# Two states per partition in a selective scan: half blocks, column-half sums and residuals on TensorE, on one Trainium2 core

## What is computed

```python
h = _L0_tok_ref(log_dt, Lambda, x, 1024)          # (64, 128, 1024): a kernel of 1024 lengths per head
h = concatenate([h, txt], axis=1)                 # (64, 205, 1024)
h = h + attn(layernorm(h))
h = h + ffn(layernorm(h))

def attn(x):                                      # selective scan, 16 states per channel
    A = -exp(A_log)                               # (1024, 16)
    xp = einsum('bld,rd->blr', x, x_proj_w)       # 32 for dt, 16 for B, 16 for C
    dt = softplus(einsum('blr,dr->bld', xp[..., :32], dt_proj_w) + dt_proj_b)
    # for each l:  h = exp(dt * A) * h + dt * B * x ;  y = sum over the 16 states of h * C
    return y + D * x

def ffn(x):                                       # weights are looked up, 4 bits or 8 bits by row norm
    return where(norm(x) > 64, x @ w8.T, x @ w4.T) + bias
```

## Time and profile before

| | us |
|---|---|
| median of 3 runs | 6210.84 (6210.68 to 6211.06) |
| profiled execution | 6212.96 |
| its span | 6211.1 |
| PE busy | 5793.1 (93%) |
| POOL busy | 5709.9 (92%) |
| DVE busy | 5698.9 (92%) |
| ACT busy | 5123.3 (82%) |

### The profile page before, as it was taken

One profiled execution on the slowest core, in us unless ns is written; L12 is line 12 of the kernel. 1 busy time (PEld: TensorE's weight loads), 2 busy tenths in 40 slices (PEclk: granted clock), 3 DMA queues, 4 the chain that ended last, 5 costly groups with the idle time before them and its releaser, 6 DMA issues. The chain is left out here.

```text
span 6211.1 us, 111922 instructions
## 1 busy us (share of the span) xinstructions
PE 5793.1 (93%) x35091; PEld 5384.9 (87%) x35091; DVE 5698.9 (92%) x4564; ACT 5123.3 (82%) x12831; POOL 5709.9 (92%) x3484
## 2 busy tenths in 40 slices
PE   4676999999999999999999999999999999999998
PEld 3545899999999999999999999999999999999997
DVE  8776999999999999999999999999999999999996
ACT  5716888888888888888888888888888888888884
POOL 4526999999999999999999999999999999999995
PEclk9887999999999999999999999999999999999999
DMA  4701221222122211222122212221222112221220
GB/s 94 160 2 66 83 82 61 77 88 87 60 77 86 88 71 68 83 88 77 61 83 88 82 62 77 88 83 61 77 88 88 68 71 83 88 77 61 83 82 34
DMA packets 115881, 478.49 MB, mean 77 GB/s; under 512 B 17441, under 2 KB 52401, under 8 KB 107122
## 3 DMA queue, kind: packets, MB, share of 16 engines
q1 hardware_dynamic: 115314, 471.10, 22.0%
HBM read 327.82 MB, written 143.24 MB: 76 GB/s over the span
## 5 line engine op out<-in xcount | busy, mean ns | idle before, releaser
L1103 POOL TENSOR_TENSOR s_ring<-s_bc,s_u_t 128x820 f32<-128x820 f32 x2048 | 3618.3, 1788 | 4.4 <-DMA s_bc<-rows_bc 4.4
L999 ACT ACTIVATE s_decay<-s_dt_t,a_neg 128x205 f32<-128x205 f32 x8192 | 3047.3, 420 | 418.4 <-DVE s_ring L1164 346.7
L895 PE MATMUL s_y_ps<-s_ring,ident 128*128 128x205 f32 x16384 | 3140.5, 341 | 115.3 <-issue 61.6
L895 PEld LDWEIGHTS s_y_ps<-s_ring,ident 128*128 128x128 f32 x16384 | 2863.3, 191 | 207.4 <-POOL s_ring L1109 115.4
L1158 DVE TENSOR_TENSOR_SCAN s_decay<-s_decay,s_ring 128x820 f32<-128x820 f32 x1216 | 2265.0, 1863 | 192.9 <-ACT s_decay L999 178.9
L1109 POOL TENSOR_TENSOR s_ring<-s_ring,s_bc 128x820 f32<-128x820 f32 x832 | 1605.3, 1929 | 78.3 <-DVE s_ring L1158 78.2
L1158 DVE TENSOR_TENSOR_SCAN s_ring<-s_decay,s_ring 128x820 f32<-128x820 f32 x832 | 1542.8, 1854 | 41.9 <-ACT s_decay L999 41.1
L928 PE MATMUL s_xch<-s_x_t,w_low 128*128 128x205 f32 x8192 | 1524.3, 338 | 0.5 <-ACT s_x_t L1042 0.2
L928 PEld LDWEIGHTS s_xch<-s_x_t,w_low 128*128 128x128 f32 x8192 | 1422.6, 190 | 35.3 <-issue 30.5
L1164 DVE TENSOR_TENSOR s_ring<-s_decay,s_bc 128x820 f32<-128x820 f32 x1216 | 1229.5, 1011 | 41.8
L889 PE MATMUL s_y_ps<-s_x_t,s_d_diag 128*128 128x205 f32 x1024 | 279.1, 354 | 35.2 <-ACT s_x_t L1037 35.2
(11 more groups left out here) (165 smaller groups left out, 4223.5 us busy)
## 6 DMA issues: line engine op xcount, KB each, us to landing
s_bc<-rows_bc SPq DMA_DIRECT2D x64, 3280.0 KB, 11.0
mixed<-t_res SPq DMA_DIRECT2D x32, 1024.0 KB, 9.6
s_x_in<-mixed SPq DMA_DIRECT2D x64, 512.0 KB
s_h<-mixed SPq DMA_DIRECT2D x64, 512.0 KB
before<-s_h SPq DMA_DIRECT2D x64, 512.0 KB
out<-s_h SPq DMA_DIRECT2D x64, 512.0 KB
s_x_in<-in_txt SPq DMA_DIRECT2D x64, 308.0 KB
s_h<-in_txt SPq DMA_DIRECT2D x64, 308.0 KB
```

The costliest lines, as they stand in the source:

```text
L895: last = nc.tensor.matmul(y_ps, ident[:, :], ring[:, c % RING, n * LEN:(n + 1) * LEN], start=False, stop=(c % 4 == 3 and n == CN - 1))
L999: last = A.activation(decay[s % 2][:, n * LEN:(n + 1) * LEN], dt_t[:, par, j, :], ACT.Exp, scale=t["a_neg"][:, j, n0 + n:n0 + n + 1])
L1103: nc.gpsimd.tensor_tensor(ring[:, s % RING, :].rearrange("p (n l) -> p n l", n=CN), bc[:, par, n0:n0 + CN, :], u_t[:, j, :].unsqueeze(1).b ...
```

## The change

1. A partition now holds one of 64 channels for one of two neighbouring states: partitions 0 to 63 the even states, 64 to 127 the odd ones. There are 16 half blocks of 64 channels and 8 pairs of states; a chunk is one half block with 4 pairs, and there are still 32 chunks of 820 columns. Chunks s and s+1 (s even) are the two half blocks of one block. `bc` has half as many rows per partition, filled by two DMAs.
2. The softplus and dt * x are computed in the old layout (`dt_n`, `u_n`), and SP copies each piece of two blocks into the new one (`dt_t`, `u_t`) by four DMAs of 64 partitions. The copy of dt leaves the first column out, which holds 1e37 from the start; `reset` is gone.
3. PE sums a pair of chunks at once, into the two column halves of the array, with a stack of two 64x64 identities as weights, one chunk later than before.
4. PE adds the residual (a product of the identity with h1) into the bank before the four transposed products, which are now products rather than transposes. ACT takes the bank to h1, for "add" with an accumulated sum, from which mean2 is made without its own pass.
5. `ON_DVE` has 23 chunks, POOL the other 9.
6. All plans, `X_ORDER` and the order of SP's queue are new.

```diff
-            sp.dma_start(t["a_neg"][:, :, :], dram["A_log"].rearrange("(j p) n -> p j n", p=P)).then_inc(alog_in, 16)
+            for i in range(2):
+                sp.dma_start(a_all[64 * i:64 * i + 64, :, :], dram["A_log"].rearrange("(b p) n -> p b n", p=64)).then_inc(alog_in, 16)
...
+PE_PLAN = {2: [("add", 0), ("ffn_late", 4)], 3: [("add", 1), ("out_low", 0)], 4: [("add", 2)], 5: [("add", 3)],
+           6: [("ffn_late", 5)], 8: [("turn1", 0)], 9: [("turn1", 1), ("ffn_late", 6)], 10: [("turn1", 2), ("turn1", 3)],
+           11: [("ffn_late", 7)], 12: [("xproj", (0, 4)), ("xproj", (4, 8))], 15: [("dt", 0)], 17: [("turn2", 0)],
+           18: [("out_low", 1), ("turn2", 1)], 20: [("dt", 1)], 22: [("out_high", 0), ("out_high", 1), ("turn2", 2)],
+           23: [("dt", 2)], 25: [("turn2", 3)], 26: [("ffn", 0), ("ffn", 1)], 28: [("dt", 3), ("ffn", 2)], 31: [("ffn", 3)]}
+ACT_PLAN = {0: [("mean1", 0)], 1: [("blk", -1), ("var1", 0)], 2: [("add", 0)], 3: [("mean1", 1), ("ffn_late", 4), ("add", 1)],
+            5: [("mean2", 0), ("out_low", 0)], 6: [("add", 2), ("var1", 1)], 7: [("blk", 0), ("norm1", 0)],
...
+            25: [("soft", (2, 1)), ("soft", (2, 2))], 26: [("blk", 5)], 27: [("ffn", 0)], 28: [("ffn", 1)],
+            29: [("soft", (3, 0))], 30: [("ffn", 2), ("soft", (3, 1)), ("blk", 6)], 31: [("soft", (3, 2)), ("ffn", 3)]}
+DVE_PLAN = {19: [("dt", 0)], 21: [("dt", 1)], 25: [("dt", 2)], 31: [("dt", 3)]}
+POOL_PLAN = {7: [("root1", 0)], 8: [("u_hi", 2)], 12: [("u_hi", 3)], 18: [("root2", 0)], 26: [("u_lo", 0)], 28: [("u_lo", 1)]}
...
+SP_ORDER = [("keep", 0), ("u_hi", 2), ("u_hi", 3), ("spread", 0), ("steps", 0), ("u_lo", 0), ("steps", 1), ("u_lo", 1),
+            ("steps", 2), ("write", 0), ("load_rows", 0), ("load", 0), ("steps", 3)]
...
-ON_DVE = (1, 3, 4, 5, 7, 9, 11, 13, 14, 15, 17, 19, 21, 23, 24, 25, 27, 29, 31)
+ON_DVE = (1, 2, 3, 5, 6, 7, 8, 9, 11, 13, 14, 15, 16, 17, 18, 19, 21, 23, 24, 27, 29, 30, 31)
...
+            def halves(target, place, source, r, first, signal):
+
+                for i in range(2):
+                    for h in range(2):
+                        sp.dma_start(target[64 * i:64 * i + 64, place + h:place + 4:2, first:],
+                                     source[64 * h:64 * h + 64, 2 * r:2 * r + 2, first:]).then_inc(signal, 16)
+
+            def steps(v, par, r):
+                wait(sp, p_empty, v * P_USES + r + 2)
+                halves(dt_t, dt_place(par, 4 * r), dt_n, r, 1, dt_in[r])
+
+            def inputs(v, r):
+                wait(sp, u_done, v * 4 + r + 1)
+                halves(u_t, 4 * r, u_n, r, 0, u_in[r])
...
                 for n in range(CN):
-                    last = nc.tensor.matmul(y_ps, ident[:, :], ring[:, c % RING, n * LEN:(n + 1) * LEN],
-                                            start=False, stop=(c % 4 == 3 and n == CN - 1))
-                last.then_inc(sum_done, 1)
+                    for h in range(2):
+                        last = nc.tensor.matmul(y_ps[sides[h], :], t["stack"][:, :], ring[:, (c + h) % RING, n * LEN:(n + 1) * LEN],
+                                                start=False, stop=(c % 4 == 2 and n == CN - 1))
+                        if n == CN - 1:
+                            last.then_inc(sum_done, 1)
...
+                nc.tensor.matmul(bank[0:rows(k), :], ident[0:rows(k), 0:rows(k)], h1[0:rows(k), par, k, 512 * side:512 * side + 512],
+                                 start=True, stop=False)
                 for j in range(4):
-                    last = nc.tensor.transpose(bank[0:rows(k), P * j:P * j + P], x_t[:, par, 4 * side + j, cols(k)], ident[:, :])
+                    last = nc.tensor.matmul(bank[0:rows(k), P * j:P * j + P], x_t[:, par, 4 * side + j, cols(k)], ident[:, :], start=False, stop=(j == 3))
...
+            def add(v, par, r, x):
+                k, side = r // 2, r % 2
+                bank, empty = take(x, "add", r)
+                A.activation(h1[0:rows(k), par, k, 512 * side:512 * side + 512], bank[0:rows(k), :], ACT.Copy,
+                             accum_out=half_sum[0:rows(k), k, side:side + 1]).then_inc(empty, 1)
```

More of the change, by code:

```diff
@@ L27 @@
 NS = 16
+NB, NK = 2 * ND, NS // 2
 RANK = 32
@@ L616, in _ @@
                 last.then_inc(turned, 1)
[L619 to L624, removed]
@@ L837, in spread @@
                 wait(sp, spread_out, v * 16 + 16)
-                sp.dma_start(bc[:, par, :, :], rows_bc[par:par + 1, :, :].broadcast_to([P, 2 * NS, LEN])).then_inc(bc_in[par], 16)
-            def entry(u, par, x, groups, ahead=True):
-                if "add" in groups:
-                    keep(u - 1, 1 - par, x)
-                if "turn1" in groups and ahead:
-                    load(u + 2, x)
-                if "turn1" in groups:
-                    spread(u + 1, 1 - par)
-                if "out_low" in groups:
-                    write(u - 2, par, x)
-                if not isinstance(u, int) or 0 <= u < BATCH:
-                    load_rows(u, par)
+                for i in range(2):
+                    sp.dma_start(bc[64 * i:64 * i + 64, par, :, :],
+                                 rows_bc[par:par + 1, i::2, :].broadcast_to([64, 2 * NK, LEN])).then_inc(bc_in[par], 16)
@@ new lines, in inputs @@
+            def inputs(v, r):
+                wait(sp, u_done, v * 4 + r + 1)
+                halves(u_t, 4 * r, u_n, r, 0, u_in[r])
+            def entry(u, par, x, groups, ahead=True):
+                for name, arg in SP_ORDER:
+                    if name == "keep" and "add" in groups:
+                        keep(u - 1, 1 - par, x)
+                    if name == "load" and "turn1" in groups and ahead:
+                        load(u + 2, x)
+                    if name == "spread" and "turn1" in groups:
+                        spread(u + 1, 1 - par)
+                    if name == "write" and "out_low" in groups:
+                        write(u - 2, par, x)
+                    if name == "load_rows" and (not isinstance(u, int) or 0 <= u < BATCH):
+                        load_rows(u, par)
+                    if name == "steps" and "turn1" in groups:
+                        steps(u + 1, 1 - par, arg)
+                    if name == "u_lo" and "turn1" in groups:
+                        inputs(u + 1, arg)
+                    if name == "u_hi" and (not isinstance(u, int) or 0 <= u < BATCH):
+                        inputs(u, arg)
@@ L884, in sums @@
                 j = c // 4
+                sides = [slice(64 * h, 64 * h + 64) for h in range(2)]
                 if c % 4 == 0:
@@ L995, in chunk @@
                     wait(act, dve_hc, u * PER_DVE + by_dve(before))
[L996 to L1000 removed]
+                if s == 0:
+                    act.wait_ge(large_set, 1)
+                if s % 8 == 0:
+                    wait(act, dt_in[s // 8], u * 64 + 64)
+                for k in range(CN):
+                    last = A.activation(decay[s % 2][:, k * LEN:(k + 1) * LEN], dt_t[:, dt_place(par, b), :], ACT.Exp,
+                                        scale=t["a_neg"][:, b, k0 + k:k0 + k + 1])
                 last.then_inc(decay_done, 1)
@@ L1008, in mean @@
                 n = rows(k)
+                minus_mean = t["ln_in"][0:n, which - 1, 0, k:k + 1]
                 if which == 1:
                     wait(act, loaded, v * 32 + 32)
+                    A.activation(xn[0:n, k, :], x_in[0:n, k, :], ACT.Copy, accum_out=ln_sum[0:n, k:k + 1]).then_inc(ln_piece[which], 1)
+                    wait(act, ln_piece[which], v * LN_DONE + PIECE[which]["mean", k, 0])
+                    A.activation(minus_mean, ln_sum[0:n, k:k + 1], ACT.Copy, scale=-1.0 / DIM).then_inc(ln_piece[which], 1)
                 else:
@@ L1032, in var, with finish @@
                 A.activation(ve, total, ACT.Identity, scale=1.0 / DIM, bias=t["eps_ln"][0:n, :]).then_inc(ln_piece[which], 1)
+            def add(v, par, r, x):
[3 more added lines that the diff above has]
+                             accum_out=half_sum[0:rows(k), k, side:side + 1]).then_inc(empty, 1)
+            def finish(name, v, par, k, x):
+                side = ("out_low", "out_high").index(name)
+                bank, empty = take(x, name, k)
+                if side == 0 and k == 0:
+                    wait(act, kept[par], (v - par) * 16 + 32)
+                A.activation(h1[0:rows(k), par, k, 512 * side:512 * side + 512], bank[0:rows(k), :], ACT.Copy).then_inc(empty, 1)
             def block_output(u, par, j, x):
```

168 lines of the change are left out of this document (77 added, 91 removed), and 6 rows, old and new, of the table ACT_PLAN.

## The result

The changed kernel takes 6716.26 us (median of 4 runs, 6713.19 to 6734.76), the kernel before 6210.76. The ratio is 1.082 (95% interval 1.0807 to 1.0833): 505 us slower, where 25 us faster was forecast, and outside the range of 6010 to 6340. The profiled execution after took 6734.76 us with a span of 6733.0.

A forecast was written before the change was run, and what follows sets the result against it. POOL was taken as the bound, 87.9 us an entry. DVE's 82.9 plus 2.0 for PE's lateness and 2.4 for the load gave 87.3; 64 entries saved 38 us, once-only costs added 13: 6185 us, range 6010 to 6340.

The forecast's parts named there:

- Engine loads: Busy time per entry after the change: DVE 82.9 us and busiest, POOL 78.3, ACT 78.9, PE 71 to 76.
- Its sums: PE's C sums in two column halves: 0.09 us a record, falling from 44.5 to 23 us an entry.
- The load of x_in: End of SP's queue: next x_in lands 1.5 us after DVE's chunk 31, idling DVE 2.4 us an entry.
- load_rows and the load behind it: Last transfers in SP's queue: 4.5 us at 367 GB/s plus 1.6 for start and landing, 6.1; slower pace 6.9.
- the eight issues ahead of the write: SP's four DMAs of u_lo 1 and four of steps 2, 0.45 to 0.54 us apart: 4.0 us.
- Rival B: SP's queue, slots 28 to 31: x_in lands at +4 or later; 6314 us at +4.0, 6371 at +4.9; chance 0.28.
- +1.7: Landing of x_in in us after DVE's chunk 31, beyond which each further us adds 64 us in total.
- +2.2: Landing of x_in in us after DVE's chunk 31 at which the entry reaches 87.9 us, deciding for Rival B.
- The other idle time: DVE idle from PE's lateness, slots 3 to 11 and 28 to 31: 2.0 us an entry, bounds 0.5 and 4.6.
- Once only: Costs outside the repeated entries: first softplus pieces +4, tail after the last scan +8, A_log load +1: +13 us.
- The clock: PE, 83% busy with short gaps, keeps its clock at 0.99 unless waits grow.
- Rival A: The load of x_in is in time: entry 84.9 us (83.5 to 85.6), total 6032 us; chance 0.28.

The follow-up runs named there:

- e5: e4 with write and load_rows moved ahead of both u_lo in SP's queue; 6158.74 us, ratio 0.9925 to the kernel before.
- e7: e5 with the C sums over the full array width, weights padded with 64 columns of zeros; 6861.07 us, ratio 1.1055.
- e3: Changed kernel with the four dt copies of steps 3 moved behind the next entry's keep, the load still late; 6616.16 us, ratio 1.0663.
- e1: Changed kernel with the load of x_in moved ahead of spread in SP's queue; 6316.58 us, ratio 1.0186.
- e4: Changed kernel with the moves of e1 and e3 together: load early, steps 3 behind the next keep; 6256.9 us, ratio 1.0081.
- e6: e5 without the residual products on PE, so the output is wrong; 6069.24 us, ratio 0.9779.
- e11: e10 with four entries in a pass of the engines' loop instead of two; 6101.3 us, ratio 0.983.
- e10: e9 with out_high 0 one slot sooner on PE, slot 21 instead of 22; 6147.9 us, ratio 0.99.
- e9: e5 with ffn_late 4 ahead of add 0 in PE's and ACT's plans and in X_ORDER; 6148.95 us, ratio 0.9904.

## Why the prediction was wrong

**Engine loads: right but for PE.** DVE, POOL and ACT came within 0.4 us an entry. PE has 81.3 us, and 79.3 in e5 with fewer stops, instead of 71 to 76. Its sums take 1718.6 / 64 = 26.9 of them in e5 where 23 was taken; which of its other terms make up the rest was not worked out. PE had room for it. (Its records were 5638 / 11.36 = 496 an entry by the earlier trace rows, not 512.) The sums come 16 records in 1.56 us, 0.10 each with the end of the last one in it, about the 0.09 taken. The Trainium skill's sentence that a weight load overlaps matmuls in flight only where the row group differs (TensorE: Matmul & The Clock Gate, Part 3) doesn't hold here: both halves use all rows, and e7 and e5 differ by 2.94 against 1.56 us for 16 records, each with its own load.

**The load of x_in: right in place, wrong in size. This is the failed step.** The step is the term "load_rows and the load behind it", 6.1 us that measured 10.75, and in second place the eight issues ahead of the write, 4.0 that measured 5.5. The terms by the rows of SP's queue above, counted from 3003.68:

| | forecast | measured |
|---|---|---|
| u_lo 1 issued | -12.9 | -12.7 |
| eight copies issued | 4.0 | 5.5 |
| write to load_rows | 4.3 | 4.3 |
| load_rows and load landed | 6.1 | 10.75 |
| x_in there | +1.5 | +7.9 |

These two carry all of it. The issues were priced by whole-tile DMAs, 0.45 each, but a copy over 64 partitions takes (2993.69 - 2991.02) / 4 = 0.67 to the next. Even the high bound, 0.7, would have done for that one. The transfer was priced at 367 GB/s, the best pace of large rows with nothing else under way, and its high bound of 6.9 was still 3.9 short. Of the 4.6 us that are missing from 6.1, the four copies of steps 3 behind the load take 1.8 (e3). The other 2.8 remain in e3 too; load_rows and the load are four issues that take 3003.30 - 3000.81 = 2.5 us before the last of them is even sent, and the sum had no such term, though the rows had the lengths of such issues (0.80 for two, 0.35 for one). That these 2.5 us are in the 2.8 is argued, not tried.

**Rival B was the mechanism, outside its bounds.** By its own sum an entry at +7.9 is 82.9 + 1.5 + 8.8 = 93.2, and the time 6211 + 64 x 5.3 + 13 = 6563; the other 153 us are idle time elsewhere. Its highest point was +4.9, since the transfer stood in it with a bound that was too narrow. Its rule, 64 us for each us later than +1.7, makes (7.9 - 1.7) x 64 = 397 us, and e1 gives back 400, but this agreement is luck: e1 takes away the whole stop of 8.8 us, 563 us, and other waits take some 160 back. The +1.7 is worked out nowhere, and the +2.2 counts 2.0 us of lateness where the sum at +4.0 counts 1.5.

**The other idle time: some 5 us an entry where 2.0 was taken.** DVE stands 96.3 - 82.5 = 13.8 us an entry (96.3 is between the two counts), 8.8 of it behind x_in. Its parts, as far as runs separate them: copies of steps 3 in the way of the next entry's first chunks (e4 against e1, 60 us), the late write and rows (e5 against e4, 98 us), the residual products (e6, 90 us), and the loop's turn (e11 against e10, 47 us for half of the turns). They overlap: what the residual products cost, they cost at the turn. The turn was in the kernel before too: its writes at 3040.95 and 3129.93 lie 89.0 apart, the next 86.5, and so on in turn, 89.6 and 86.4 on average. I divided 2000 us by 22.75 entries and didn't look at them one by one, so the new sum, built from DVE's load, has no term for it.

Without load and turn, the entries of e5, whose engine plans are the forecast's, take 84.1 us on average, and those of e9 85.2, where the sum had 84.9. So the forecast of what the engines can do was good to 1 us in 85 away from the turn; SP's queue, 32 copies and eleven other transfers an entry, took it back.

**Once only: +13 taken.** In the profiled executions the spans differ by 521.9 us; less 64 x 8.2 or 8.6 (entries of 96.1 or 96.5) that leaves -3 to -29. The last entries have no load to wait for; that this is the whole difference was argued, not tried.

**The clock: only as a consequence.** I wrote that it keeps 0.99 unless waits grow. They did, and the mean over the span fell from 0.978 to 0.904. What this costs by itself wasn't separated from the waits that cause it; in e9 the clock rose by 0.010 and the time fell by 10 us.

**Rival A** (6032, the load in time) is what e1 makes of the kernel, and it came to 6317. DVE's 8.8 us gave back 400 / 64 = 6.2: other late things, among them the stops of ACT ("issue", still 45.2 us in e1), had stood in the shadow of the load. Of the versions with a right output only e11 (6101) comes near A's 6032.

## What to carry to other kernels

Price a queue that works in order as you would an engine: every issue at its own length, every transfer against those that share the DMA engines with it, and the slack of what stands last. Before the arithmetic of engines is trusted to 1%, list what an in-order queue passes in the last fifth of a period and who waits for it; here a list's order was worth 558 us, and with the best order tried the whole change gains 49 (e5). Look at single periods, not only their mean: an alternation of 3 us showed a cost of the loop that a mean hides. And count a stop by its place, not only by the name that the list of waits gives it: one stop had two names here.

## What the runs showed of the hardware that I had not expected

**TensorE's clock falls in a stop and stays low for the work that ends it.** Short stretches at the end of another entry (the same columns as the stretch above), after:

```profile
3102.00:3103.00 1.00, 0.00 (x0) 0.00 (x0) 0.00 (x0) 0.55 (x2) 0.52 (x1) 1.00 0.98 228
3103.00:3104.00 1.00, 0.00 (x0) 0.00 (x0) 0.00 (x0) 0.00 (x0) 0.00 (x0) 0.92 0.91 221
3104.00:3105.00 1.00, 0.00 (x0) 0.00 (x0) 0.00 (x0) 0.00 (x0) 0.00 (x0) 0.50 0.75 165
```

PE had stood since 3100.95. The granted clock goes to 0.50, 1.2 GHz, and is at 0.98 again only in the stretch from 3114 to 3116. The add that comes next, and the same work at 2.4 GHz a few us later, after:

```profile
3110.71 2.07 PE L974 MATMUL s_xch<-s_h,ident 128*128 128x512 f32 x2 [9.76 <-ACT s_x_t L1122]
3112.58 1.78 PE L977 MATMUL s_xch<-ident,s_x_t 128*128 128x128 f32 x8
...
3116.98 1.02 PE L974 MATMUL s_xch<-s_h,ident 128*128 128x512 f32 x2
3117.83 1.05 PE L977 MATMUL s_xch<-ident,s_x_t 128*128 128x128 f32 x8
```

The add takes 3.65 us instead of 1.90, just where ACT waits for it.

**Where the loop goes round, ACT stops at chunk 0 for 2.0 to 2.7 us in every kernel, and for longer when bulk transfers are in flight.** ACT in the entry of those stretches, after:

```profile
3101.41 1.14 ACT L1068 ACTIVATE s_decay<-s_dt_t,a_neg 128x205 f32<-128x205 f32 x3 [4.16 <-issue]
3107.27 0.43 ACT L1068 ACTIVATE s_decay<-s_dt_t,a_neg 128x205 f32<-128x205 f32 x1 [4.72 <-issue]
```

The second stop lies inside one chunk, between exponentials that wait for nothing. In 3 of the 10 such entries between 2000 and 4000 us such stops hide the wait for x_in whole, as here; in the others a part of it is left. In the same place, before:

```profile
3068.26 1.50 ACT L999 ACTIVATE s_decay<-s_dt_t,a_neg 128x205 f32<-128x205 f32 x4 [2.39 <-issue]
```

And ACT with DVE's product of chunk 30, the one that ACT has to wait for at chunk 0, e5:

```profile
3029.35 0.43 ACT L1143 ACTIVATE s_y_t<-s_xch,y_bias 128x205 f32<-128x205 f32 x1 [0.75 <-PE s_xch L996]
3032.22 1.14 ACT L1070 ACTIVATE s_decay<-s_dt_t,a_neg 128x205 f32<-128x205 f32 x3 [2.44 <-DVE s_ring L1240]
```

```profile
3027.54 1.01 DVE L1240 TENSOR_TENSOR s_ring<-s_decay,s_bc 128x820 f32<-128x820 f32 x1
```

The product ended at 3028.55, before ACT was free (3029.78), so the 2.44 us are the same stop under another name. Counting every stop of 1.5 us or more ahead of the exponentials from 2000 to 4000 us, under either name, there are 26.1 us in 12 turns of the loop before (2.2 each), 67.4 in 10 after (6.7), 51.1 in 12 in e4 (4.3), 27.6 in 11 in e5 (2.5) and 14.6 in 6 in e11 (2.4). So some 2.4 us belong to the turn, and what the late transfers add to it is gone in e5. The page of the profile counts packets of a kind "instruction" on the DMA engines, 368 and 235 in the changed kernel (6.03 and 1.93 MB), 342 and 362 in e11 with its longer loop, so code does pass through the engines that the bulk keeps busy. That ACT's stops are waits for such packets fits this, but no run shows it.
